# Additive attention: GpSimd holds one relu back behind VectorE's five, and the denominator is read one slot later

## What is computed

```python
q = jnp.einsum('bnc,ac->bna', X, Wq)          # A = 64 features
k = jnp.einsum('bnc,ac->bna', X, Wk)
Vy = jnp.einsum('bnc,dc->bnd', X, Wy_w) + Wy_b
e = jax.nn.relu(_rho_signed_sqrt(q[:, :, None, :] + k[:, None, :, :]))
scores = jnp.einsum('bija,a->bij', e, Wphi)
ex = jnp.exp(scores - jnp.max(scores, axis=-1, keepdims=True))
denom = jnp.sum(ex, axis=-1)
part1 = jnp.einsum('bij,bjc->bic', ex, Vy)
Ew = jnp.einsum('bij,bija->bia', ex, e)
part2 = jnp.einsum('bia,ca->bic', Ew, We_w) + We_b * denom[..., None]
return (part1 + part2) / (denom[..., None] + EPS_DEN)
```

## Time and profile before

| | |
|---|---|
| median of 3 runs | 5183.36 us (5178.34 to 5184.76) |
| profiled execution | 5164.71 us, span 5163.0 us, mean granted TensorE clock 0.944 |
| busy: TensorE / VectorE / ScalarE / GpSimd | 4455.2 / 4160.2 / 3438.4 / 3240.4 us |
| attention phase (weightings L796) | from 1244 to 4441 us of the span |
| weightings L796, 2048 | 2391.6 us busy |
| VectorE's relus L753, 635 | 649.2 us busy |
| roots L585, 512 | 1854.8 us busy |
| GpSimd's clamps L681 and adds L687, 889 each | 1032.0 and 1010.3 us busy |

### The profile page before, as it was taken

One profiled execution on the slowest core, in us unless ns is written; L12 is line 12 of the kernel. 1 busy time (PEld: TensorE's weight loads), 2 busy tenths in 40 slices (PEclk: granted clock), 3 DMA queues, 4 the chain that ended last, 5 costly groups with the idle time before them and its releaser, 6 DMA issues.

```text
span 5163.0 us, 83882 instructions
## 1 busy us (share of the span) xinstructions
PE 4455.2 (86%) x28586; PEld 2326.0 (45%) x28586; DVE 4160.2 (81%) x6598; ACT 3438.4 (67%) x2402; POOL 3240.4 (63%) x2716
## 2 busy tenths in 40 slices
PE   6888877887888888888888888888888888799998
PEld 3333333564333333333433433343343334577777
DVE  2789796536999999999999999999999999522225
ACT  2223122215889988889888888988888898534343
POOL 1676572534777777777777777777777777243334
PEclk8888787898999999999999999999999999999999
DMA  6000001351000000000000000000000000200002
GB/s 224 0 0 1 0 1 65 133 184 55 3 2 3 3 2 2 19 2 2 4 2 2 17 4 2 2 4 2 11 3 5 2 2 4 99 17 8 16 25 82
DMA packets 70510, 131.01 MB, mean 25 GB/s; under 512 B 8264, under 2 KB 46632, under 8 KB 65889
## 3 DMA queue, kind: packets, MB, share of 16 engines
q1 hardware_dynamic: 61152, 106.21, 6.0%
q0 software_dynamic: 9216, 23.17, 1.2%
HBM read 74.66 MB, written 61.03 MB: 26 GB/s over the span
## 4 chain that ended last, share of the span: by engine, by line
DVE 44%; issue 19%; PE 17%; POOL 3%; DVEq 1%; ACT 1%; DMA 0%; POOLq 0%; SPq 0%; ACTq 0%
DVE e_slots L796 27%; DVE e_slots L753 10%; PE banks L2250 6%; PE banks L492 2%; DVE ew L796 2%; POOL g_l L2380 2%; PE banks L451 2%; PE banks L1602 1%; DVE half_max L760 1%; PE banks L288 1%; PE banks L1553 1%; PE banks L1656 1%; PE banks L1665 1%; DVEq L794 0%; PE banks L1587 0%
## 5 line engine op out<-in xcount | busy, mean ns | idle before, releaser
L796 DVE CUSTOM_DVE_ANT_0 e_slots<-e_slots,banks 128x1024 f32<-128x1024 f32 x2048 | 2391.6, 1213 | 79.4 <-PE banks L492 78.4
L585 ACT ACTIVATE e_slots<-e_slots 128x4096 f32<-128x4096 f32 x512 | 1854.8, 3624 | 230.7 <-DVE e_slots L753 174.4
L492 PE MATMUL banks<-ex_parts,sel 128*128 128x512 f32 x4096 | 1507.1, 455 | 373.1 <-DVE ew L796 327.3
L681 POOL TENSOR_SCALAR e_slots<-k,qt 128x1024 f32<-128x1024 f32 x889 | 1032.0, 1163 | 670.1 <-DVE ew L796 623.4
L451 PE MATMUL banks<-e_slots,w_score 128*32 128x256 f32 x16384 | 1207.8, 396 | 73.2 <-ACT e_slots L585 73.1
L492 PEld LDWEIGHTS banks<-ex_parts,sel 128*128 128x128 f32 x4096 | 640.6, 193 | 1149.3 <-DVE ew L796 930.5
L687 POOL TENSOR_SCALAR e_slots<-e_slots,qt 128x1024 f32<-128x1024 f32 x889 | 1010.3, 1148 | 51.2 <-POOL e_slots L681 25.5
L451 PEld LDWEIGHTS banks<-e_slots,w_score 128*32 128x32 f32 x16384 | 392.8, 110 | 725.0 <-issue 482.2
L753 DVE TENSOR_SCALAR e_slots<-k,qt 128x1024 f32<-128x1024 f32 x635 | 649.2, 1086 | 0.0
L576 ACT ACTIVATE e_slots<-k,qt 128x1024 f32<-128x1024 f32 x508 | 568.3, 1136 | 9.5 <-DVE ew L796 5.1
L2380 POOL TENSOR_TENSOR g_l<-tmp,g_h 128x512 fp32r<-128x512 f32 x192 | 259.6, 1352 | 420.6 <-ACT g_h L2347 288.7
(11 more groups left out here) (341 smaller groups left out, 5025.9 us busy)
## 6 DMA issues: line engine op xcount, KB each, us to landing
stage<-in_h SPq DMA_DIRECT2D x16, 1024.0 KB, 4.8
moe_slots<-empty_slot SPq DMA_DIRECT2D x1, 10320.0 KB, 33.3
slots<-moe_slots SPq DMA_DIRECT2D x8, 1290.0 KB, 6.6
moe_out<-empty_slot SPq DMA_DIRECT2D x1, 8192.0 KB, 53.4
two_rows<-moe_out SPq DMA_DIRECT2D x16, 512.0 KB, 5.8
stage<-in_w SPq DMA_DIRECT2D x6, 1024.0 KB, 6.2
x_tokens<-in_x SPq DMA_DIRECT2D x1, 4096.0 KB, 18.7
w_down<-in_w_down SPq DMA_DIRECT2D x1, 4096.0 KB, 12.9
```

Source lines behind the costliest of these rows:

```text
L492: ins = nc.tensor.matmul(spread[n % 2][:, half * W:(half + 1) * W], c_["sel"][:, half, n, :], ex_parts[:, par, :], start=True, stop=True)
L585: nc.scalar.activation(e_slots[:, par, four, :], e_slots[:, par, four, :], ACT.Sqrt, bias=EPS_RHO).then_inc(sqrt_done, 1)
L681: nc.gpsimd.tensor_scalar(e_slots[:, par, n, :], k2[:, :], FLT_MAX, qt[:, par, 1, place(n):place(n) + 1], ALU.min, ALU.max).then_inc(z_cla ...
L796: nc.vector.tensor_tensor_reduce(out=e, in0=e, in1=spread[n % 2], scale=1.0, scalar=0.0, op0=ALU.mult, op1=ALU.add, accum_out=ew[:, q, pla ...
```

## The change

Two places. In GpSimd's step a wait on `z_v` is put ahead of the pair of slot 15: VectorE has made five relus a tile, and with (t + 3) x 5 counted it has also made those of tile t + 2. In VectorE's step `group_end(ends, 0)` moves from slot 12 to slot 13.

```diff
                 pool.wait_ge(bc_done, t * NP)
                 parts(t + 1, 1 - par)
                 if not last:
+                    pool.wait_ge(z_v, t * Z_BY.count("V") + 3 * Z_BY.count("V"))
                     some_z(t + 2, par, (15,), t * NP)
@@
                     if seam is not None and n == SEAM_AT:
                         next_batch(seam)
-                    if ends is not None and n == MAX_AT + 2:
+                    if ends is not None and n == MAX_AT + 3:
                         group_end(ends, 0)
```

## The result

The change made the kernel **5.1% faster**: 4912.3 us median of 4 runs (4905.39 to 4919.31), for 5180.85 us before (4 runs); the ratio is 0.9487, 95% interval 0.9463 to 0.9512. The forecast was 4963 us with a range from 4915 to 5055. The direction and the mechanism were as foretold; the gain was 269 us instead of 220. The median stands 3 us under the low end, and the ratio applied to the 5183 us that the prediction started from gives 4917 us, 2 us above it: the result is at the edge of the range, not near the forecast.

A forecast was written before the change was run, and what follows sets the result against it. VectorE was taken to bound the attention phase, busy 3121.78 of 3197 us. The terms −220 + 6 + 8 + 26 − 40 gave −220 us, so 5183.4 us would become 4963, range 4915 to 5055.

The forecast's parts named there:

- (a): VectorE's relu block: two relus no longer collide with GpSimd's pair of slot 15, 1.75 us a block, −220 us.
- (b): Next step: GpSimd runs 0.85 us late behind its new wait, costing +6 us for blocked relus and +8 through ScalarE's root.
- (c): Fourth step of a group: TensorE's pair of spreads for the third slot starts 0.8 to 0.9 us late, +26 us.
- (d): TensorE's clock: its fall to 0.50 about once a group mostly goes as the standstill shortens, −40 us.
- (e): VectorE's read of the denominator, one slot later: same price once a group, 0 us.
- Rival 1: TensorE's clock still falls once a group: −180 us, 5003 us; chance 0.18.
- Rival 2: Every step pays (c), GpSimd, ScalarE and TensorE each having under 0.5 us of slack: 5029 us; chance 0.10.
- Rival 3: GpSimd becomes the bound, its L667 and L669 slipping into the relu block: 32 us slower, 5215 us; chance 0.03.
- Rival 4: The relus are slow for another reason, such as what ScalarE's root reads; all stays at 5183 us; chance 0.03.
- Rival 5: No stall of (b) and (c) and no clock fall left: −280 us, 4903 us; chance 0.04.

The follow-up runs named there:

- e4: Changed kernel, but GpSimd's pair of slot 15 waits for two of the five relus instead of all five; 0.9671 of the time before.
- e7: Changed kernel, but GpSimd's pair of slot 15 waits for the first weighting of the next step; 0.9648 of the time before.
- e8: Kernel before, with TensorE repeating its slot 1 pair of spreads three, four, three and two extra times in a group's steps; 0.9932.
- e5: Kernel before, with TensorE repeating its slot 1 pair of spreads twice more in three steps of a group, once in the fourth; 0.9959.
- e1: Changed kernel with the denominator read where it was, so GpSimd's new wait alone; 0.9485 of the time before.
- e2: Kernel before with only the denominator's read moved one slot later; 0.9999 of the time before.
- e3: Changed kernel, but GpSimd's pair of slot 15 waits for four of the five relus; 0.9438 of the time before, 4886.7 us.
- e9: Changed kernel, but GpSimd's pair of slot 15 waits for three of the five relus; 0.9456 of the time before.

## Why the prediction was right, and where not

**(a) The collision: right.** −220 us forecast, 217 measured in busy time, with equal spacings of 0.66 us and each of GpSimd's instructions back at 1.12. The trace had shown the cause; e4 confirmed it by moving the slow relu from the second and third place to the fifth.

**(b) GpSimd's lateness: the chain right, the size too large.** I reckoned 0.85 us behind the third clamp and charged 14 us. That clamp is 0.64 us late (+5.49, for +4.85), and the third step is 22.36 us, 1.73 less than before, so nothing was paid there. The term that was mis-sized is, for the most part, the copy L691: I took its 0.67 us as its length, when it too had been issued beside relus, and it came down to 0.21. (Of the 0.46 us, 0.27 came back as a longer wait of the clamp behind it and 0.03 as its own later start, so the first clamp is 0.16 us earlier than I had it.) Then ScalarE's exp was 0.25 us late in the short steps, and L669 with it, not 0.45 to 0.85, which keeps L669 out of the block. The root of slots 8 to 11 began at −0.77 us before the third step and ended at +2.85, before TensorE wanted it; before the fourth it began at −0.52, as I had it, and ended at +3.10, and there TensorE came to its scores only at +3.22. e7 shows that the chain itself is as described, that a late L669 does block the first relu, and that lateness costs nearly one for one once there is more of it.

**(c) TensorE in the fourth step: the place right, the size wrong.** +26 us forecast, 5 measured (0.16 us in some 31 steps). The pair of spreads starts at +1.58, for +1.27 before: 0.31 us late, not 0.8 to 0.9. The root of slots 4 to 7 was 0.25 us late, not 0.5. And the slack was larger than the 1.33 us that I took: that idle time counts from the recorded end of L464, 0.70 us behind its start, but L464 holds up the next pair by 0.35 us only (2802.95 to 2803.30), so the slack was some 1.68 us, and 1.68 − 1.75 − 0.25 = −0.32. I also added 0.25 us for the slots behind, where nothing was lost. This is the larger part of what was missed.

**(d) The clock: right in size.** −40 us forecast, 43 measured; e8 shows the cause apart from the relus. With the rule of the Trainium skill (TensorE: Matmul & The Clock Gate, Part 1), that activity is what holds the full clock, the trace agrees in direction; by it I had put all 48 us as gone, and 13 us stayed. Which standstills make a fall can't be told from these runs: e5 only moved them.

**(e) The denominator: 0 forecast, −3.5 us by the steps' lengths** of e1 and e2 against their partners, nothing in the runs. The step that failed is small: I kept the price of the read whole, but the weighting behind the row maximum now follows it by 0.06 us instead of 0.15.

The sum: −218 by the spacings, 0, +5, −43, −3 and −2 at the ends of batches make −261 for −220. Of the 41 us between them, 35 are stalls that I charged under (b) and (c) and that didn't come. The range reached down to the result only because its low end charged nothing for either: the mechanism was right, and the size of the gain was met at the edge. The median's gain of 269 us has some more, of the size by which single runs differ outside this phase (16 us between the two profiled executions).

**The rivals.** Rival 1 (a fall once a group stays) and 2 (every step pays) are out, by the steps' lengths. Rival 3 (GpSimd becomes the bound) is out, yet e7 found its slope: GpSimd 1.1 us later is 1.7% of the time (0.9648 for 0.9487). Rival 4 (another reason for the slow relus) is out by e4. Rival 5 (no stall and no fall left, 4903 us), to which I gave 0.04, came nearest, nearer than the forecast with its 0.62; the measured time lies between the two, and e3 goes beyond it with 0.9438, which is 4892 us of the 5183 that the prediction started from.

## What to carry to other kernels

When equal instructions of one engine have unequal lengths, set the starts of the other engines' instructions beside them before anything else: here VectorE's relus and GpSimd's elementwise work excluded each other, and one wait on an engine with idle time took 217 us off the engine without any. Place such a wait as early as it still works: with four of five relus counted the clamp is issued while the last one runs, which gave another half a percent; three counted did about as well (0.9456), but two cost 1.9% against the change (0.9671 for 0.9487), so the margin is one relu. And when a collision is priced, take every instruction of the waiting side that falls beside it at its undisturbed length, the small ones too, and read what an instruction holds up from the spacing to the next, not from its length.

## What the runs showed of the hardware

- The exclusion isn't symmetric in what one instruction loses. A GpSimd clamp issued beside a row of relus spaced 0.66 us waited 0.81 us, through the end of one and all of the next, in e4 and e9, and 0.23 us behind the last; a relu behind a clamp that had begun lost 0.87 us in the kernel before (spacing 1.53 for 0.66) and 0.78 us in e4 (length 1.53 for 0.75). The last 0.19 us of a GpSimd instruction didn't block: L669 in e7 ended 0.37 us past a relu's dispatch and cost it 0.18.
- The same exclusion hit a copy of 32 columns, 0.67 us beside the relus and 0.21 without them, while VectorE's weightings, which read one operand from PSUM, hardly felt GpSimd: in the kernel before, the 696 of them between 1300 and 4100 us with GpSimd busy beside 95% or more of their length took 1214 ns on average, and the 179 with none of it beside them 1209.
- TensorE's clock fell to 0.50 (1.2 GHz) after standstills of 1.95 and 0.41 us in the kernel before, and of 1.45 and 0.41 in e5; in the changed kernel it also fell where no standstill but those of 0.49 and 0.51 us stood right ahead. Filling a standstill with repeated matmuls gave 0.7% in e8.
